# Scan stage of a four-layer kernel: the transposed tile sum is multiplied with its gate by VectorE, straight from PSUM, in place of a ScalarE copy and a GpSimd product

## What is computed

```python
def step(state, inp):
    dt_t, B_t, C_t, u_t = inp
    dA = jnp.exp(dt_t[..., None] * A)
    state = state * dA + (dt_t * u_t)[..., None] * B_t[:, None, :]
    y = jnp.einsum('bdn,bn->bd', state, C_t)
    return (state, y)
...
y = ys.transpose(1, 0, 2) + x * D
y = y * jax.nn.silu(gate)
return y @ W_out.T
```

## Time and profile before

| | us |
|---|---|
| median of 3 runs | 1749.05 (1748.15 to 1751.51) |
| the profiled execution, whole | 1750.26 |
| its span, first to last instruction | 1748.5 |
| VectorE's first scan starts | 177.45 |
| VectorE's last scan starts | 501.48 |
| first instruction of the next stage's ScalarE | 509.79 |

### The profile page before, as it was taken

How to read it: one execution, slowest core, us unless ns; L and a number is a source line. 1 busy time by engine, 2 the same in 40 slices (tenths; PEclk the granted TensorE clock), 3 DMA queues, 4 the chain that set the end, 5 groups by cost and what they waited for, 6 DMA issues and landing times. The chain is left out here.

```text
span 1748.5 us, 25644 instructions
## 1 busy us (share of the span) xinstructions
PE 1618.7 (93%) x8758; PEld 1379.1 (79%) x8758; DVE 1118.6 (64%) x1580; ACT 895.7 (51%) x1905; POOL 802.8 (46%) x458
## 2 busy tenths in 40 slices
PE   5995999999978799999979999999999998899998
PEld 3862899999967588778868988888888887788876
DVE  4327999999976223365527677676767768755422
ACT  2336888888754344335425554545445454533321
POOL 2212899999965363335213332333223333466343
PEclk9998999999989899999989999999999998999999
DMA  3201010102020573002100010000100012144100
GB/s 118 67 1 58 1 46 10 55 0 103 1 97 1 215 268 130 18 1 91 37 25 25 25 49 24 24 24 27 45 24 24 30 55 73 37 156 163 42 19 30
DMA packets 25195, 97.79 MB, mean 56 GB/s; under 512 B 3104, under 2 KB 3360, under 8 KB 22688
## 3 DMA queue, kind: packets, MB, share of 16 engines
q1 hardware_dynamic: 24976, 96.75, 15.5%
q10 hardware_dynamic: 144, 0.07, 0.0%
HBM read 94.57 MB, written 2.23 MB: 55 GB/s over the span
## 5 line engine op out<-in xcount | busy, mean ns | idle before, releaser
L863 POOL TENSOR_TENSOR scratch_s<-scratch_s,scan_cm 128x1024 f32<-128x1024 f32 x96 | 227.4, 2369 | 25.5 <-DVE scratch_s L1035 25.4
L1861 POOL TENSOR_TENSOR stretch_turned<-stretch_turned,res_const 128x1024 f32<-128x1024 f32 x32 | 77.4, 2419 | 226.5 <-ACT stretch_turned L1704 226.5
L1547 PE MATMUL psum<-opnd_xh,query_wqh 128*128 128x256 f32 x512 | 151.6, 296 | 1.9 <-PEq L94 1.9
L1129 PE MATMUL psum<-res_const,scratch_s 128*128 128x128 f32 x1088 | 144.7, 273 | 2.2 <-POOL scratch_s L863 2.2
L1547 PE MATMUL psum<-opnd_xl,query_wqh 128*128 128x256 f32 x512 | 145.7, 285 | 0.0
L1547 PE MATMUL psum<-opnd_xh,query_wql 128*128 128x256 f32 x512 | 145.7, 285 | 0.0
L1129 PEld LDWEIGHTS psum<-res_const,scratch_s 128*128 128x128 f32 x1088 | 128.7, 141 | 18.3 <-POOL scratch_s L863 2.4
L1712 ACT ACTIVATE stretch_pa<-psum,stretch_nm 128x128 f32<-128x128 f32 x128 | 45.2, 365 | 159.5 <-DVE stretch_nm L1966 159.5
L919 ACT ACTIVATE scratch_s<-ssm_dt,ssm_vec 128x255 f32 (+1 forms) x256 | 112.4, 500 | 11.0 <-DVE scratch_s L1035 8.4
L1123 PE MATMUL psum<-scan_diag,scratch_s 128*128 128x256 f32 x448 | 111.8, 385 | 6.7 <-ACT scratch_s L911 6.7
L1123 PE MATMUL psum<-diag_odd_diag,scratch_s 128*128 128x256 f32 x448 | 110.0, 380 | 0.0
(11 more groups left out here) (332 smaller groups left out, 4749.9 us busy)
## 6 DMA issues: line engine op xcount, KB each, us to landing
mi_dw<-in_dw SPq DMA_DIRECT2D x24, 448.0 KB, 7.0
mi_dm<-in_dm SPq DMA_DIRECT2D x24, 448.0 KB, 7.3
query_raw<-in_w_q SPq DMA_DIRECT2D x8, 1024.0 KB, 4.7
query_raw<-in_w_o SPq DMA_DIRECT2D x8, 1024.0 KB, 4.8
gu_raw<-in_w_gu SPq DMA_DIRECT2D x11, 512.0 KB, 4.8
mlpa_raw<-in_w_mlp SPq DMA_DIRECT2D x7, 768.0 KB, 4.4
mlpa_base<-in_b_mlp SPq DMA_DIRECT2D x7, 768.0 KB, 6.0
mlpb_raw<-in_w_mlp SPq DMA_DIRECT2D x7, 768.0 KB, 4.2
```

Of the source, the lines that this page charges most:

```text
L863: nc.gpsimd.tensor_tensor(slot[h][r], slot[h][r], weights(4 * h, 4), ALU.mult).then_inc(weighted_pool, 1)
L1129: mm = nc.tensor.matmul(ps_y[:, t * P:(t + 1) * P], part[:, t * P:(t + 1) * P], ident, start=start and t == 0, stop=stop and t == QT - 1, ...
L1547: mm = nc.tensor.matmul(ps_q[:, h * SEQ:(h + 1) * SEQ], w[:, k, h * HD:(h + 1) * HD], x[:, k, b * SEQ:(b + 1) * SEQ], start=(k == 0 and w ...
L1861: nc.gpsimd.tensor_tensor(heads(turned[:, :]), heads(turned[:, :]), over_heads(C_SIN, SEQ), ALU.mult).then_inc(q_sine, 1)
```

## The change

ScalarE's `finish` and GpSimd's `gating` go, with the semaphore `gated`. VectorE gets a `finish` that multiplies the turned sum in PSUM with the gate in SBUF and writes `flat_x`; it stands ahead of the scan p = 6 of the next tile, behind the second `weigh`. TensorE's waits on `finished` stay as they are and are now answered by VectorE.

```diff
-            def gating(s):
-                pool.wait_ge(finished, s + 1)
-                nc.gpsimd.tensor_tensor(flat_x[:, cols(s, SEQ)], flat_x[:, cols(s, SEQ)], flat_gate[:, cols(s, SEQ)],
-                                        ALU.mult).then_inc(gated, 1)
...
                     weigh(s, r, 1, b)
-                    if not first:
-                        gating(s - 1)
...
             weigh(TILES - 1, 1, 2, BATCH - 1)
-            gating(TILES - 1)
-            pool.wait_ge(gated, TILES)
...
-            def finish(s):
-                act.wait_ge(y_back, s + 1)
-                nc.scalar.activation(flat_x[:, cols(s, SEQ)], ps_back, ACT.Copy).then_inc(finished, 1)
...
                     decay_pair(s, r, 6)
-                    if not first:
-                        finish(s - 1)
...
             keep(TILES - 1)
-            finish(TILES - 1)
...
+            def finish(s):
+                dve.wait_ge(y_back, s + 1)
+                nc.vector.tensor_tensor(flat_x[:, cols(s, SEQ)], ps_back, flat_gate[:, cols(s, SEQ)], ALU.mult).then_inc(finished, 1)
+
             def body(b, j, switch):
                 for r in range(2):
                     s = b * KI + j * 2 + r
+                    first = isinstance(s, int) and s == 0
                     recur_first(s, r)
                     for p in range(PAIRS):
                         if p - 1 in OWN_AT:
                             weigh_ready(s, OWN_AT.index(p - 1), b)
+                        if p == PAIRS - 1 and not first:
+                            finish(s - 1)
                         recur(s, r, p)
...
             pairs(dve, body)
+            finish(TILES - 1)
+            dve.wait_ge(finished, TILES)
```

More of the change, by code:

```diff
@@ L740, in scan_phase @@
     summed, summed_pool, finished, skip_ready = sem("summed"), sem("summed_pool"), sem("finished"), sem("skip_ready")
-    gated = sem("gated")
     bm_in, cm_in, raw_ready, squared, mean_ready, eps_added = (sem("bm_in"), sem("cm_in"), sem("raw_ready"), sem("squared"),
```

## The result

The changed kernel takes 1756.65 us in the median of 6 runs (1755.11 to 1758.66), against 1749.34 for 6 runs of the kernel before (1747.44 to 1751.51). The ratio is 1.0039 with a 95% interval of 1.0029 to 1.0049: +7.3 us in the medians, 5.1 to 8.6 by the interval, where +6.5 was forecast. The profiled execution took 1756.54 us.

A forecast was written before the change was run, and what follows sets the result against it. TensorE's 10.20 us per tile was taken to bound the later scan tiles, just above VectorE's 10.09. The terms 9.6 - 2.3 - 0.8 = +6.5 us on 1749.05 gave 1755.6 us, range 1752.0 to 1759.8.

The forecast's parts named there:

- VectorE becomes the bound: Scan stage: with the product VectorE needs 10.40 us per tile, slower than TensorE's 10.20, and sets the pace.
- The price, 0.31 us, 31 times: VectorE's new 128x256 product, 31 of them ahead of a scan: +9.6 us (9.0 to 12.1).
- TensorE's pace gives back 2.3 us: Scan stage: VectorE's present waits for TensorE's slower pace go, -2.3 us (0 to -2.3).
- Nothing from ScalarE and GpSimd: Scan tiles: dropping L907 (0.26 us) and L854 (0.74 us) gains 0, as both engines wait anyway.
- The added wait is free: VectorE's wait on `y_back` ahead of the product: sum ready 2.1 us early, cost 0.
- The end gains 0.8: End of the scan stage: 1.18 us of copy and product become one record of 0.39, -0.8 us (0 to -0.8).
- a nearly free product: Rival: a product priced under TensorE's lead of 0.11 us per tile hides, only the end gains; 1748.3 us, 5%.
- No overlap: Rival: each product on VectorE costs its whole record, 31 x 0.39 = 12.1, net +9.0, 1758.0 us; 14%.
- the estimate beside that rival: Trainium skill's formula (N + 151) / 0.96 ns for the product: 31 x 0.42 = 13.1 us, total near 1759.
- A late `y_back`: Rival: back transposes land after the product's place; each 0.1 us beyond the margin costs 3.1, 1758.7 at 0.1; 4%.
- The mean granted clock: Rival: TensorE's granted clock shifts outside the measured stretches, moving the time by up to 3.9 us, 1751.7 to 1759.5; 7%.

The follow-up runs named there:

- psum_mid: Changed kernel with VectorE's product from PSUM moved to right behind the scan p = 5; 1757.05 us, 1.0040 of the kernel before.
- before_p4: Changed kernel with the product two scans earlier, ahead of the scan p = 4; 1756.84 us, 1.0035 of the kernel before.
- last_only: Kernel before with only the last of the 32 tiles finished by VectorE from PSUM; 1749.04 us, 0.9991 of the kernel before.
- before_p3: Changed kernel with the product ahead of the scan p = 3, before the sum is back; 1788.65 us, 1.0215 of the kernel before.
- from_sbuf: Changed kernel, but ScalarE's copy kept and VectorE's product reading both inputs from SBUF; 1757.99 us, 1.0039 of the kernel before.
- sbuf_mid: from_sbuf with the product moved right behind the scan p = 5, amid GpSimd's weighing; 1776.86 us, 1.0148 of the kernel before.

## Why the prediction was right

By its own steps:

- *VectorE becomes the bound.* Shown. The tiles are of equal length, TensorE follows at 10.42 where it ran at 10.20, doubling the product costs its spacing in full, and GpSimd, ScalarE and TensorE's weight loads wait for VectorE's scans. The picture of the kernel before was right in the pace and too simple in the place: VectorE's second scan comes after 1.27 us or more in five of the later tiles and not in every second one, and from tile 24 on the wait stands ahead of the scan p = 5 instead, which starts 1.22 to 1.33 us after the one before it in every second tile.
- *The price, 0.31 us, 31 times.* It measured 0.33, so +10.2 instead of +9.6. This is the one term that was mis-sized. The product was priced from L1043, which stands behind a scan and takes 0.58; the new product stands behind L1043. Behind a scan the same product takes 0.31, but then what stands behind it takes 0.02 more: L1043 takes 0.60 in place of 0.58 (psum_mid), a scan 1.13 in place of 1.11 (before_p4). So the product adds 0.33 to a tile wherever it stands, and 10.42 comes out in each order. The prediction had left out what a product does to its successor, though the kernel before shows it: its scans take 1.12 to 1.13 behind L1043 and 1.11 behind a scan. The sizes give 0.065 fixed plus 1.04 ns per column behind a product: 0.07 for 8, 0.195 for 128, 0.33 for 256.
- *TensorE's pace gives back 2.3 us.* Shown. The tiles before and after account for it: 315.07 + 30 x 0.33 - 322.67 = 2.3. The run with 8 columns shows the same lead from the other side, a product of 0.07 that costs nothing. The size is that of one execution: it hangs on the lead, and with the later rise of the clock in last_only VectorE's waits were 0.85 us longer.
- *Nothing from ScalarE and GpSimd.* Shown by the run that cut their work in the kernel before: 315.05 against 315.07.
- *The added wait is free.* Shown, and with more margin than was read from the kernel before. There it was 2.1 us; with TensorE no longer late the sum is back at 308.42 and the product starts at 311.50, 3.1 us later.
- *The end gains 0.8.* It gained 0.64. ScalarE's and GpSimd's 1.18 became one record of 0.42, but VectorE starts 0.73 after the start of the back transposes where ScalarE started after 0.66, and the barrier took 1.27 instead of 1.22. The 0.07 goes with the clock, 0.50 at the transposes after and 0.60 before; in last_only, at 1.00, VectorE started after 0.47.
- The rivals: a nearly free product exists, but only below 0.1 us (8 columns). "No overlap" did not come true: the product's record is 0.41, close to the 424 ns of the estimate beside that rival, but the next scan starts 0.33 after the product's start, and with 128 columns 0.20 after the start of a record of 0.28. The section of the Trainium skill that the prediction names there, "The DRAIN you can't avoid" in "VectorE: DVE Perf Modes", goes on to say that a next instruction that is not held starts earlier; the 0.33 agrees with that part. A late `y_back` costs what the prediction said, its lateness in each tile (before_p3), but the margin kept it away. The mean granted clock of the profiled pair, 0.977 after and 0.978 before, did not shift by enough to see; the 1.36 us behind the stage are within the scatter of one kernel's runs (1755.11 to 1758.66).

The sum for the stage was 9.6 - 2.3 - 0.8 = 6.5, and its terms measured 10.2 - 2.3 - 0.6 = 7.3. The total came close because each term was near its size, not because large errors cancelled.

## What to carry to other kernels

Two operations of 1.1 us in sum on engines that wait anyway are cheaper than one of 0.33 us on the engine that sets the pace. When two engines are both full, find which sets the pace by the spacing of a repeated instruction, early and late in the stage: the difference between the two paces (here 0.11 us per tile) is all that a new instruction on the other one may cost, and the lead that hides it changes with the clock at the start of the stage. Price a new instruction by start-to-start spacing behind the same kind of neighbour, and keep products with two SBUF inputs out of the way of GpSimd.

## What was not expected of the hardware

A VectorE product with both inputs in SBUF that starts inside a GpSimd product does not show as idle time but as a longer record. The later GpSimd's record ends, the longer it gets, and it ends 0.28 or 0.29 us after GpSimd's each time:

| GpSimd's record ends after the product's start by | product's record | where |
|---|---|---|
| 0.13 | 0.42 | from_sbuf, 301.47 |
| 0.37 | 0.66 | sbuf_mid, 526.72 |
| 0.63 | 0.92 | from_sbuf, 437.00 |
| 0.71 | 0.99 | sbuf_mid, 306.12 |
| 1.05 | 1.34 | sbuf_mid, 449.28 |

A record of the undisturbed length, 0.41 to 0.42, is as long as 0.13 + 0.28, so at 0.13 there is nothing left to see. What happens in those 0.28 us was not tested.

The price of a short product depends on its neighbour and is in part paid by its successor: 0.31 us behind a scan, 0.33 behind another product, and the instruction behind it takes 0.02 more than behind a scan.

TensorE's granted clock differed between executions at the two ends of the stage, where the kernels do the same, and 0.2 to 0.9 us went with it. At the start it rose from 0.50 to 1.00 before 180 us in the kernel before and only at 182 in last_only, and TensorE's lead differed by 0.8 us. At the end the last transposes took 0.44 where it was still 1.00, and 0.63 to 0.69 where it had fallen to 0.60 or 0.50.
